# Value products of two attention layers as three fp32r matmuls, sums of exponentials as a row moved by DMA, and an order of work with every step moved singly

## What is computed

```python
# layer 0: group norm (8 groups), then full attention over 1024 positions, width 128
attn = softmax(q @ k.T * C ** -0.5); out = (attn @ v) @ Wp.T + bp; x = out + xn
# layer 1: group norm (32 groups), attention with 8 heads of width 16, projection, residual
# layer 2: instance norm, full attention over 1024 positions, width 128, residual
# layer 3: linear attention with normalised q and k of width 16, scaled by gamma
```

## Time and profile before

| what | value |
|---|---|
| median of 3 runs | 7174.82 us |
| lowest, highest | 7168.03, 7176.58 us |
| the profiled execution: its own time | 7171.95 us |
| its span (first to last recorded instruction) | 7170.2 us |
| TensorE busy | 6650.7 us, 93% |
| VectorE busy | 3877.9 us, 54% |
| ScalarE busy | 3528.2 us, 49% |
| GpSimd busy | 1986.0 us, 28% |

### The profile page before, as it was taken

The page is one execution under the profiler, slowest core; times in us unless marked ns, Lnnn a source line. Parts: engine busy times, 40 slices in busy tenths (PEclk is TensorE's granted clock), DMA queues, the critical chain, the costliest instruction groups (busy, mean ns, idle before and its releaser), DMA issues.

```text
span 7170.2 us, 77303 instructions
## 1 busy us (share of the span) xinstructions
PE 6650.7 (93%) x30286; PEld 2982.2 (42%) x30286; DVE 3877.9 (54%) x4531; ACT 3528.2 (49%) x4548; POOL 1986.0 (28%) x1585
## 2 busy tenths in 40 slices
PE   5799999999999999999999999999999999999986
PEld 2344444444444444444444444444444444444333
DVE  2555555555555555555555555555555555555541
ACT  1455445555445555455555455555455555455442
POOL 2122233222232222232222232222233222233212
PEclk7999999999999999999999999999999999999987
DMA  1010100110100110100110100110100110100000
GB/s 31 13 22 16 25 22 13 25 25 16 25 22 13 25 25 16 25 22 13 25 25 16 25 22 13 25 24 16 25 22 13 25 23 17 25 22 13 22 13 7
DMA packets 68108, 144.68 MB, mean 20 GB/s; under 512 B 32672, under 2 KB 34848, under 8 KB 67616
## 3 DMA queue, kind: packets, MB, share of 16 engines
q1 hardware_dynamic: 67744, 139.73, 8.4%
HBM read 18.07 MB, written 16.78 MB: 5 GB/s over the span
## 4 chain that ended last, share of the span: by engine, by line
PE 76%; DVE 9%; issue 6%; ACT 3%; SPq 2%; POOL 2%; DMA 2%; POOLq 0%; DVEq 0%; ACTq 0%
PE p_chain L1048 18%; PE p_max L1048 14%; PE p_sc L1048 13%; PE p_full L1048 11%; PE p_acc L1048 11%; PE p_head L1048 8%; DVE mx_half L899 4%; DMA qs<-neg 2%; SPq L524 1%; POOL t_rn L642 1%; DVE f2mx L894 1%; SPq L522 1%; DVE f0mx L894 1%; ACT p L763 1%; ACT exact L686 1%
## 5 line engine op out<-in xcount | busy, mean ns | idle before, releaser
L899 DVE TENSOR_REDUCE mx_half<-p_max 128x2 f32<-128x1024 f32 x2048 | 2506.8, 1224 | 1928.4 <-PE p_max L1048 1928.2
L763 ACT ACTIVATE p<-p_head 128x1024 f32<-128x1024 f32 x2048 | 2096.1, 1023 | 1954.5 <-PE p_head L1048 1939.6
L631 POOL TENSOR_TENSOR fsum<-fsum,fp 128x512 f32<-128x512 f32 x768 | 978.5, 1274 | 1498.6 <-ACT fp L740 1486.1
L1048 PE MATMUL p_max<-ks,qs 63*128 63x512 f32 x4096 | 1032.1, 500 | 89.6 <-DVE mx_half L899 77.5
L1048 PE MATMUL p_acc<-p,v 128*32 128x512 f32 x8192 | 1108.8, 611 | 1.3 <-ACT p L763 1.1
L1048 PE MATMUL p_head<-qs,ks 64*128 64x512 f32 x4096 | 977.0, 473 | 134.9 <-DMA qs<-neg 110.0
L740 ACT ACTIVATE fp<-p_sc 128x512 f32<-128x512 f32 x1024 | 612.2, 598 | 891.0 <-PE p_sc L1048 758.9
L1048 PEld LDWEIGHTS p_max<-ks,qs 63*128 63x128 f32 x4096 | 392.4, 188 | 1156.8 <-DVE mx_half L899 574.6
L1048 PEld LDWEIGHTS p_head<-qs,ks 64*128 64x128 f32 x4096 | 394.4, 189 | 804.1 <-issue 516.0
L1048 PE MATMUL p_full<-fp,f0v 128*128 128x512 f32 x1024 | 596.0, 665 | 0.0
L1048 PE MATMUL p_full<-fp,f2v 128*128 128x512 f32 x1024 | 561.7, 631 | 0.0
(11 more groups left out here) (167 smaller groups left out, 7087.8 us busy)
## 6 DMA issues: line engine op xcount, KB each, us to landing
qs<-cq_hi SPq DMA_DIRECT2D x128, 256.0 KB, 4.8
ks<-ck_hi SPq DMA_DIRECT2D x128, 256.0 KB, 4.9
x_in<-x_dram SPq DMA_DIRECT2D x32, 512.0 KB, 3.5
qs<-cq_lo SPq DMA_DIRECT2D x64, 256.0 KB, 4.4
ks<-ck_lo SPq DMA_DIRECT2D x64, 256.0 KB, 5.1
out_dram<-x SPq DMA_DIRECT2D x32, 512.0 KB, 2.7
zrow<-rz SPq DMA_DIRECT2D x128, 16.0 KB
cw<-packed_dram SPq DMA_DIRECT2D x1, 1178.0 KB, 5.1
```

What stands on the lines that cost most here:

```text
L631: pool.tensor_tensor(dst, dst, fp[u % 3][:, :], ALU.add).then_inc(f.sum, 1)
L763: act.activation(p1[slot][:, 2 * pr:2 * pr + 2, :], P_HEAD[:, :].rearrange("p (e n) -> p e n", e=2), ACT.Exp, scale=float(DH) ** -0.5).the ...
L899: dve.reduce_max(mx_half[:, pr, :, t, kh], P_MAX[:, :].rearrange("p (e n) -> p e n", e=2), AX.X)\
L1048: return pe.matmul(dst, lhsT, rhs, start=start, stop=stop)
```

## The change

- **f_pv**: each exponential and each value is now kept as two fp32r parts. ScalarE makes the exponential twice (fp_hi rounded to fp32r, fp exact), GpSimd subtracts them (`f_plo` gives fp_lo), and the product is three fp32r matmuls. There are two buffers of each in place of three.
- **f_keep** reads P_CHAIN twice (hi, then `exact`), and GpSimd's `f_vlo` subtracts. P_CHAIN is handed on after the second reading.
- **f_sums**: two fp32 matmuls with one column of ones as weights and 512 moving columns; `f_row` (ScalarE) copies each result row of 1x512 into x3; `f_gather` (DMA) brings the row onto 128 partitions, `f_recip` takes reciprocals and splits them in hi and lo on VectorE, `f_return` (two DMAs) puts them back as two rows, and **f_spread** is one fp32r matmul per half.
- **s_pv** writes 17 rows per head instead of 32. One matmul at the start clears P_ACC.
- `f_shift` writes a buffer per half that both layers share.
- **template**: all of PLACE has new numbers, and the scores, maxima and units get an offset each (HEAD_MOVE, MAX_MOVE, FULL_MAX_MOVE, FULL_MOVE).

On SyncE's queue a period now stands in this order: f_return (layer 0), load, stack (g = 0), m_row (g = 1), o_gather, o_return, f_gather and f_return (layer 2), stack (g = 1), o_gather, m_row (g = 0 of the next image), o_return, store, f_gather (layer 0).

```diff
-                    t = PLACE['h0'] + PLACE['hp0']*v if r < 2 else PLACE['h1'] + PLACE['hp1']*(v-4*T)
+                    t = (PLACE['h0'] + PLACE['hp0']*v if r < 2 else PLACE['h1'] + PLACE['hp1']*(v-4*T)) + HEAD_MOVE[v]
...
+            def f_gather(b, layer):
+                sp.wait_ge(f.zrow, b.at(PER.f_zrow, 2))
+                sp.dma_start(f_zt[layer][:, :], sums_row(layer)).then_inc(f.zt, 16)
+            def f_return(b, layer):
+                sp.wait_ge(f.r, b.at(PER.f_r, 1))
+                after(sp, (f.rb, b.shift(-1), PER.f_rb, 2))
+                for part in range(2):
+                    row = FULL_ROW[layer] + part
+                    sp.dma_start(f32(zrow[row:row + 1, :]), f32(f_rz2[layer][:, part, :]))\
+                        .then_inc(f.row, 16)
...
+            def f_plo(b, u, layer):
+                pool.wait_ge(f.p, b.at(PER.f_p, u + 1))
+                pool.wait_ge(f.pexact, b.at(PER.f_pexact, u + 1))
+                pool.tensor_tensor(fp_lo[u % 2][:, :], fp[u % 2][:, :], f32(fp_hi[u % 2][:, :]),
+                                   ALU.subtract).then_inc(f.plo, 1)
...
-                act.activation(fp[u % 3][:, :], P_SC[:, :], ACT.Exp,
-                               scale=float(C) ** -0.5).then_inc(f.p, 1)
+                act.activation(fp_hi[u % 2][:, :], P_SC[:, :], ACT.Exp,
+                               scale=float(C) ** -0.5).then_inc(f.p, 1)
+                if u >= 2:
+                    act.wait_ge(f.sum, b.at(PER.f_sum, sums_through(u - 2)))
...
+                act.activation(fp[u % 2][:, :], P_SC[:, :], ACT.Exp,
+                               scale=float(C) ** -0.5).then_inc(f.pexact, 1)
...
-                pe.wait_ge(f.p, b.at(PER.f_p, u + 1))
+                pe.wait_ge(f.plo, b.at(PER.f_plo, u + 1))
...
-                mm(P_FULL[:, :], f_v[layer][:, kt, :], fp[u % 3][:, :], start=kt == 0,
-                   stop=kt == T - 1).then_inc(f.pv, 1)
+                hi, lo = (v[:, kt, :] for v in f_v[layer])
+                mm(P_FULL[:, :], hi, fp_hi[u % 2][:, :], start=kt == 0, stop=False)
+                mm(P_FULL[:, :], hi, fp_lo[u % 2][:, :], start=False, stop=False)
+                mm(P_FULL[:, :], lo, fp_hi[u % 2][:, :], start=False, stop=kt == T - 1)\
+                    .then_inc(f.pv, 1)
...
-                for t in range(T):
-                    last = mm(P_CHAIN[:, t:t + 1], fsum[:, tile(t)], ones[:, 0:1])
-                last.then_inc(f.z, 1)
+                mm(P_CHAIN[0:1, :], ones[:, 0:1], fsum[:, half(h)]).then_inc(f.z, 1)
...
-                for t in range(T // 2):
-                    s = 4 * h + t
-                    last = mm(P_CHAIN[:, tile(t)],
-                              f_recip[layer][:, s:s + 1].broadcast_to([C, C]), mat("ident"))
-                last.then_inc(f.rb, 1)
+                mm(P_CHAIN[:, :], ones_r[r, :], zrow[r, half(h)]).then_inc(f.rb, 1)
```

More of the change, by code:

```diff
@@ L113 @@
     f_vout = 2
+    f_vexact = 2
+    f_vlo = 2
     f_tile = T
@@ L118 @@
     f_p = 2 * T
+    f_pexact = 2 * T
+    f_plo = 2 * T
     f_pv = 2 * T
@@ L193, in __init__ @@
         self.vout = new(f"f{layer}_vout")
+        self.vexact = new(f"f{layer}_vexact")
+        self.vlo = new(f"f{layer}_vlo")
         self.tile = new(f"f{layer}_tile")
@@ L198, in __init__ @@
         self.p = new(f"f{layer}_p")
+        self.pexact = new(f"f{layer}_pexact")
+        self.plo = new(f"f{layer}_plo")
         self.pv = new(f"f{layer}_pv")
@@ L202, in __init__ @@
         self.z = new(f"f{layer}_z")
+        self.zrow = new(f"f{layer}_zrow")
+        self.zt = new(f"f{layer}_zt")
+        self.dve = new(f"f{layer}_dve")
         self.r = new(f"f{layer}_r")
+        self.row = new(f"f{layer}_row")
         self.rb = new(f"f{layer}_rb")
@@ L345, in heads_kernel @@
         ks = sb("ks", [C, PAIRS, N], F32R)
[L346 removed]
+        v1 = [sb(f"v1_{i}", [C, T, HEADS, DH + 1]) for i in range(2)]
         mx_half = sb("mx_half", [C, PAIRS, 2, T, 2])
@@ L390, in full, with sums_row @@
             return sem.f0 if layer == 0 else sem.f2
+        def sums_row(layer):
+            row = 0 if layer == 0 else 32
+            return x3[row:row + 1, :]
         def col(name, width=1):
@@ L646, in _ @@
             play(pool, dict(g_var=g_var, p_var=p_var, i_stat=i_stat, f_lo=f_lo, p_lo=p_lo,
-                            f_shift=f_shift, f_add=f_add, f_out=f_out, t_norms=t_norms))
+                            f_shift=f_shift, f_vlo=f_vlo, f_plo=f_plo, f_add=f_add, f_out=f_out, t_norms=t_norms))
         @block.scalar
@@ L1248, in f_spread @@
             def f_spread(b, h, layer):
-                f = full(layer)
+                f, r = full(layer), slice(FULL_ROW[layer], FULL_ROW[layer] + 2)
                 if h == 0:
-                    pe.wait_ge(f.r, b.at(PER.f_r, 1))
+                    pe.wait_ge(f.row, b.at(PER.f_row, 32))
+                    if layer == 0:
+                        after(pe, (sem.f2.vexact, b.shift(-2), PER.f_vexact, 2),
+                              (sem.f0.zrow, b, PER.f_zrow, 2))
+                    else:
+                        pe.wait_ge(sem.f2.zrow, b.at(PER.f_zrow, 2))
```

238 lines of the change are left out of this document (150 added, 88 removed), and 8 rows, old and new, of tables (HEAD_MOVE, MAX_MOVE).

## The result

The changed kernel takes 6744.73 us (median of 4 runs, 6740.0 to 6745.8), the one before 7174.4 us. The ratio is 0.9401, with an interval of 0.9385 to 0.9417. The forecast was 6760 us. The profiled execution took 6743.66 us, 1.9 us more than its span. Two executions, one of e5 at 11260.92 us and one of the kernel before at 7489.31 us, were in a slower state, and the ratios leave them out.

The account below looks back on a forecast made before the run. TensorE, busy 93% of the span, was taken as the bound. 7172 - 174 (products) - 85 (spreads) + 16 (sums) - 154 (borders) - 77 (shift row) - 112 (clock) + 160 (waits) + 15 (ends) = 6761, forecast 6760 us, range 6630 to 7040.

Parts of the forecast that it names:

- value products: f_pv on TensorE: 1024 products go from one fp32 matmul to three fp32r passes, 0.17 us less each, -174 us.
- spreads and sums: Softmax sums and spreads on TensorE: spreads as one fp32r pass, -85 us; sums as two fp32 products per layer, +16 us.
- borders: TensorE changes between 64-row and all-row steps: 24 fewer per image at 0.2 us each, -154 us.
- clock: TensorE's granted clock behind the one-column sums and the shift-row wait: 3.5 of 6 us per image given back, -112 us.
- ends: Fill and drain: longer last-image chain (row copy, DMA trips, small operations) and looser order, +15 us.
- TensorE's own work: TensorE's work per image falls from about 200 to 187 us.
- the lower bound of the gain: Value product at 0.91 us if the last fp32r pass pays more, a gain of 0.15 us each.
- The shift row: First scores of layer 1 waiting for m_row's DMA: about 1.0 of 3.4 us per image is left, -77 us.
- The new waits: TensorE waits at P_CHAIN, f_max of layer 0 and pairs of s_scores: 5 us per image, +160 us.
- the clock stays: Rival: the fall behind the sums is unrelated to them and returns elsewhere; 1 of 3.5 us comes, 6840 us; chance 0.12.
- The waits eat it: Rival: P_MAX and P_CHAIN chains keep their length; 11 us new waits per image, clock returns 1 us, 7030 us; chance 0.28.
- Slower: GpSimd's queue: Rival: f_plo held behind waiting t_norms delays f_pv, 14 us per image over the forecast, 7210 us; chance 0.08.

Follow-up runs that it names:

- e5: Kernel before with only the value products changed to three fp32r passes and what feeds them, in the old order (also 17-row s_pv, shared f_shift buffers): 7613.24 us, ratio 1.0604.
- e1: Changed kernel with each value product as one fp32 matmul again, low part of the values left out, all other steps kept: 6842.71 us, ratio 0.9536.
- e3: Kernel before with the new order of work (PLACE and offsets) and none of the new arithmetic: 6844.46 us, ratio 0.9541.
- e7: Kernel before with the sums' eight matmuls on 64 equal columns of ones in place of one: 7102.06 us, ratio 0.9893.
- e6: Changed kernel with the old one-column sums, reciprocals and fp32 spreads, in the new order (order and products without the row): 6879.65 us, ratio 0.9585.
- e9: The products-only kernel in the old order (e5) with f_out issued ahead of a subtraction and addition on GpSimd: 7403.04 us, ratio 1.0316.
- e12: Kernel before with 17 rows per head in s_pv in place of 32 and P_ACC cleared once: 7170.89 us, ratio 0.9995.

## Why the prediction was right, and where only its total was

The total was within 15 us, and that is partly luck. The waits were put 105 us too high, and the gains of the order's own work (32 us), the products (15) and the clock (11) and the cost of the ends (30) were all off to the other side. The parts, against the accounting above (us in all):

| term | predicted | measured | from |
|---|---|---|---|
| value products, own work | -174 | -159 | e1 to after |
| spreads and sums, own work | -69 | -71, with the 17 rows in it | e3 to e1 |
| borders, own work of the order | -154 | -122 | before to e3 |
| clock | -112 | -101 | half the lower clock |
| shift row and new waits (idle) | +83 | -22 | idle per image |
| ends | +15 | +45 | time less 32 periods |

**TensorE's own work** was the strongest part: 187 us per image predicted, 188.6 measured. Three passes for one fp32 product cost 0.91 us between short steps, against 0.88: the last pass pays more, as the lower bound of the gain had it. These are rows of e1 (fp32) and of the changed kernel, each product with what follows it:

```profile
3052.40 1.02 PE L1158 MATMUL p_full<-fp,f0v_hi 128*128 128x512 f32 x2
3053.35 0.50 PE L1158 MATMUL p_max<-ks,qs 63*128 63x512 f32 x2
...
3065.13 1.12 PE L1158 MATMUL p_full<-fp,f0v_hi 128*128 128x512 f32 x2
3066.18 0.51 PE L1158 MATMUL p_max<-ks,qs 63*128 63x512 f32 x2
```

```profile
3011.72 0.40 PE L1158 MATMUL p_full<-fp_hi,f0v_hi 128*128 128x512 f32 x1
...
3012.51 0.50 PE L1158 MATMUL p_max<-ks,qs 63*128 63x512 f32 x2
```

Between two 64-row steps a product went from 1.06 to 0.90 us, behind a full step and before a 64-row one from 0.95 to 0.79, between two full ones from 0.86 to 0.69. Measured over the steps around it, at the 28 of 32 places where the waits are alike in both traces, the gain is 0.12 to 0.18 us, mostly 0.15 or 0.16. So the neighbours don't matter, and 1024 times 0.155 are the 159 us of e1. The forecast's bounds (0.15 and 0.16) were right; the 0.17 that it took lies above both. The sums cost 1.90 us a layer, not 2.12: a narrow fp32 product took 0.95, between my 0.85 and 1.06. The spread, 0.40, was 0.43 in the forecast. The borders gave 3.8 us per image for 4.8; with the 28 borders that e3 saves this is 0.14 us each, not 0.2, within the 1 or 2 us that the accounting is good to. The Trainium skill ("FP8 and Floating Point Precision", TensorE Precision Notes) counts four passes for true FP32. The estimate that the prediction made from its pages was 221 us for the products; the trace has 159.

**The shift row.** The step said that 1.0 us of 3.4 is left. Nothing is left, in the changed kernel as in e3. The reasoning about the queue held, and so did the cover: 3.4 us lie between the end of m_turn's step and the first scores, where I counted 3.2. What was wrong is the price of the DMA, 4.2 us. In the changed kernel the row is issued at 3033.99, and the scores start 2.95 us later without a wait:

```profile
3033.99 0.58 SPq L579 DMA_DIRECT2D qs<-neg  x1
...
3036.94 0.50 PE L1158 MATMUL p_head<-qs,ks 64*128 64x512 f32 x2
```

The packets of the two traces show the reason. The row is 32 packets of 512 bytes. Before, they run from 3004.16 to 3004.59 us, 3.4 us after the issue, just as the last 4096-byte packet of the stack ends (3004.21). In the changed kernel they run from 3035.20 to 3035.68, 1.2 us after the issue. It is so in every image, and the kernel before has its own control: its other row (g = 1) has no stack ahead of it and starts 1.2 us after its issue too. The windows just behind the two issues (before, then after) differ in the DMA share, 0.97 and 0.05:

```profile
3000.80:3003.90 3.10, 0.83 (x4) 0.36 (x2) 0.00 (x0) 0.68 (x2) 2.22 (x2) 1.00 0.97 202
```

```profile
3034.00:3036.00 2.00, 2.00 (x9) 0.96 (x7) 0.59 (x3) 0.71 (x2) 1.43 (x2) 1.00 0.05 10
```

So the stack delayed the row twice before: at the issue, which I priced, and by its data on the DMA engines, which I took for the row's own time. The row (g = 1) behind six DMAs is hidden as well.

**The new waits** are the step that failed: +160 us for 5 us per image. The changed kernel waits less than the one before (9.70 against 10.39 us), and without the 3.4 us of the shift row that is 2.7 us of new waits, about half of what I took. I had put them at P_CHAIN, f_max and pairs of scores, and charged them to the new arithmetic. What rose is above all the wait for mx_half, VectorE's reading of P_MAX for layer 1, from 1.1 to 3.5 us per image, which I had not named; the wait of layer 2's f_max for f2mx rose from 1.2 to 2.2, and all those at P_CHAIN together fell from 3.4 to 2.0. e3 shows both rises without any new arithmetic.

**The clock** came out near its price, 101 us for 112 (rather less, as e7 shows), but not as two halves that both vanish. e7 shows the sums' half: 76 us by itself after its own cost. With order alone (e3) the clock never falls in the steady part. With the products the falls behind the sums come back (e6), the row takes these away, and 4.78 us are left in another stretch. So part of the rival "the clock stays", that a fall comes back at another place, did happen. The Trainium skill ("TensorE: Matmul & The Clock Gate", HAM oscillation) lets the clock fall after idle gaps. The spell at 3077 us agrees in so far as there is idle time ahead of it: the window in which it starts holds 2.90 us of work in 3.40. The spell behind the sums of before does not: TensorE was busy for 3.20 of 3.20 us, and e7 took it away without touching idle time.

**The waits eat it** (7030 us) didn't happen in the full change, but it did in e6, where 4.7 us of own work turned into 0.6 us more of period. **Slower: GpSimd's queue** didn't happen in the new order. In the old one, with my places for the new steps, e5 shows its kind of hold-up with the parts exchanged (f_out behind f_plo), and e9 takes a part of it away with one moved step (7.2 us of period). I had priced it at 14 us per image; idle time and half the lower clock are 35.8 us in e5 and 15.9 before, 20 us more.

What was right by balance and not by insight is the split. I read the order as borders and the shift row, 231 us with its share of the clock besides, and the arithmetic as the rest. The runs give 332 us to the order alone and 100 us to all new arithmetic, of which 230 us had been own work on paper. The difference went into the clock (77 us, from 0.00 to 4.78 us of lower level), idle time (23 us) and the ends (30 us). Of the ends' 45 us, 15 are in e3 already. The traces place them. Up to the seventh normalisation of x_in the changed kernel is 31 us faster than the one before, where six periods would give 89; behind the last one it is 32 us faster, where one period would give 15. So against the kernel before it is the start that got dearer, not the end. Against e3 most of the difference (19 of 28 us on the profiled executions) does lie behind the last normalisation, 619 us for 604; that the trip of the row through DMA and back is the reason is argued, not tried.

**Open.** Why one-column sums let the clock fall in the old surrounding and in e6, and not in e3, which differs from e6 in the products and what feeds them (and in 17 rows of s_pv); what single offsets are worth over even lanes; what the row is worth by itself; and why the products need it. e6 has 2.3 us more idle time than the changed kernel. Its wait for f_num is 1.1 us per image and not among the changed kernel's waits, those for f2mx and mx_half are 0.8 and 0.6 us longer, but no run separated them.

## What to carry to other kernels

On a saturated in-order engine, price a cheaper operation together with the order that it runs in: the same products were worth -98 us in the new list with the row, +35 us in it without the row, and +435 us in the old list with places of my own, half of which one moved step took away. Before adding a step that waits to a helper engine's queue, look at what stands behind it there and who waits for that. Test the order with the old arithmetic as a run of its own, for it can carry most of a gain that looks arithmetic.

## What the runs showed of the hardware

- fp32 matmuls with one moving column, eight in a row (16 records) on a busy TensorE, were followed by 3.4 us or more at half clock in 22 of 40 cases; with 64 columns the record grew from 252 to 278 ns, no fall stood behind the sums any more and the kernel became 76 us faster (e7). The same instructions in e3, 245 ns each, were followed by no fall; in e6, in the same order but with fp32r products, they were.
- Fewer weight columns give little back. 17 in place of 32 took a step of four fp32 products from 1.00 to 0.98 us, which the time doesn't show (e12). An fp32 product of 512 columns with a single weight column took 0.95 us behind p_acc and before a 64-row product, where one with 128 took 1.06 (e1).
- A small DMA waits for the data of large ones that were issued ahead of it: the shift row's 512-byte packets started 3.4 us after their issue behind the stack, and 1.2 us after it on free DMA engines.
- A gap need not lower the clock, and it may. In the changed kernel these two windows follow each other, and the clock is 1.00 in the idle one and behind it. Yet of the 20 images 12 have a fall within 0.3 us of the end of this same wait for f2mx:

```profile
3084.80:3088.20 3.40, 1.67 (x13) 0.76 (x6) 2.32 (x3) 1.84 (x3) 1.54 (x2) 1.00 0.00 0
3088.20:3091.60 3.40, 3.40 (x13) 1.64 (x11) 2.45 (x2) 2.41 (x4) 1.02 (x1) 1.00 0.00 0
```
